# Half edge blocks instead of whole ones: how gathered rows are signalled, copied and awaited in a graph network on one core

## What is computed

```python
summed = jax.ops.segment_sum(h[src], dst, num_segments=N_NODES)   # three SAGE layers, a GCN of two, a GIN
msg_in = jnp.concatenate([nodes[row], nodes[col], edge_features], axis=-1)
messages = _mlp(msg_in, mW1, mb1, mW2, mb2)                       # the last network sums messages instead
aggregated = jax.ops.segment_sum(messages, col, num_segments=nodes.shape[0])
upd_in = jnp.concatenate([nodes, aggregated], axis=-1)
x = _layernorm(x + _mlp(upd_in, uW1, ub1, uW2, ub2))
```

## Time and profile before

| | |
|---|---|
| runs of the kernel | 5099.02 us median of 3 (5089.89 to 5105.0) |
| the profiled execution | 5097.06 us, of which the span from first to last instruction is 5095.3 us |
| busy share of the span | PE 82%, PEld 75%, DVE 64%, ACT 54%, POOL 65% |
| mean DMA traffic | 195 GB/s |
| stretches, us from the start | Sage0 111 to 940, Sage1 to 1642, Sage2 to 2235, Gcn1 to 2790, Gcn2 to 3388, Gin to 3974, Update to 5095 |

### The profile page before, as it was taken

One profiled execution on the slowest core, in us unless ns is written; L12 is line 12 of the kernel. 1 busy time (PEld: TensorE's weight loads), 2 busy tenths in 40 slices (PEclk: granted clock), 3 DMA queues, 4 the chain that ended last, 5 costly groups with the idle time before them and its releaser, 6 DMA issues. The chain is left out here.

```text
span 5095.3 us, 116107 instructions
## 1 busy us (share of the span) xinstructions
PE 4202.0 (82%) x31493; PEld 3798.6 (75%) x31494; DVE 3265.3 (64%) x6692; ACT 2762.0 (54%) x7100; POOL 3310.3 (65%) x3162
## 2 busy tenths in 40 slices
PE   2999999799997899979997455548888599999997
PEld 1899999799997888879997445536767366666665
DVE  5555555677775788857766566657777355555555
ACT  0566666455544777854443566655666244444444
POOL 2544443478773777747774777747775677777772
PEclk9999999899999999989999766679999799999999
DMA  1778787466665677758876566647777244444442
GB/s 35 214 250 252 252 252 248 173 232 242 231 235 211 224 257 261 259 197 275 279 266 232 162 184 184 190 143 216 224 210 205 74 118 117 117 119 119 119 115 89
DMA packets 490328, 991.07 MB, mean 195 GB/s; under 512 B 156821, under 2 KB 246965, under 8 KB 470968
## 3 DMA queue, kind: packets, MB, share of 16 engines
q1 hardware_dynamic: 389368, 872.44, 50.7%
q0 software_dynamic: 100800, 116.72, 11.4%
HBM read 452.18 MB, written 380.15 MB: 163 GB/s over the span
## 5 line engine op out<-in xcount | busy, mean ns | idle before, releaser
L753 PE MATMUL ps_all<-arena 128*128 x16000 | 2023.1, 286 | 501.8 <-DMA arena<-arena 348.3
L753 PEld LDWEIGHTS ps_all<-arena 128*128 128x128 f32 x16000 | 1989.8, 204 | 549.1 <-issue 545.5
L682 POOL DMA_INDIRECT arena<-n_t,ix_now x784 | 907.8, 1158 | 426.2 <-issue 401.1
L682 POOL DMA_INDIRECT arena<-y_t,ix_now x784 | 808.3, 1031 | 347.6 <-issue 329.6
L1132 ACT ACTIVATE arena<-bytes 128x2048 f32<-128x2048 uint8 (+1 forms) x300 | 475.8, 1618 | 381.9 <-DMA bytes<-pairs_d 215.8
L682 POOL DMA_INDIRECT arena<-x_rows,ix_now x392 | 373.7, 953 | 375.1 <-PE ps_all L753 263.7
L682 POOL DMA_INDIRECT arena<-x_t,ix_now x392 | 403.7, 1030 | 176.8 <-issue 166.4
L1667 PE MATMUL ps_all<-w,tp 128*128 128x128 f32 x4000 | 490.9, 276 | 28.8 <-ACT store_b L1810 28.2
L1667 PEld LDWEIGHTS ps_all<-w,tp 128*128 128x128 f32 x4000 | 477.9, 192 | 47.2 <-issue 38.6
L1097 ACT ACTIVATE bytes<-arena 128x1024 uint8<-128x1024 f32 (+1 forms) x200 | 296.8, 1484 | 242.3 <-DMA pairs_d<-bytes 240.5
L712 DVE TENSOR_TENSOR arena<-iota,window 128x1024 f32<-128x1024 f32 x302 | 363.3, 1219 | 100.8 <-ACT bytes L1097 93.9
(11 more groups left out here) (212 smaller groups left out, 7689.5 us busy)
## 6 DMA issues: line engine op xcount, KB each, us to landing
x_t<-store_a SPq DMA_DIRECT2D x150, 512.0 KB
s_t<-store_a SPq DMA_DIRECT2D x50, 1024.0 KB
n_t<-store_b SPq DMA_DIRECT2D x50, 1024.0 KB
load_a<-s_t SPq DMA_DIRECT2D x50, 1024.0 KB
bytes<-pairs_d SPq DMA_DIRECT2D x100, 512.0 KB
y_t<-store_b SPq DMA_DIRECT2D x100, 512.0 KB
load_b<-x_t SPq DMA_DIRECT2D x100, 512.0 KB
arena<-arena SPq DMA_DIRECT2D x147, 192.0 KB
```

Of the source, the lines that this page charges most:

```text
L682: pool.indirect_dma_start(out=slot_rows(at, W, pitch), out_offset=None, in_=table, in_offset=bass.IndirectOffsetOnAxis(ap=ix_now[:, at:at ...
L753: last = pe.matmul(out(j, 2) if wide else out(j, 1), hot, both(rows) if wide else rows, start=(k == 0), stop=(k == n - 1))
```

## The change

The rows of an edge block are treated as two halves h = 0 and 1 of four tiles (`HT`), each with semaphores of its own. POOL signals each half. PE waits at group 0 of node block m only for the second half of edge block m-1, and at group 1 for the first half of edge block m. `skewed` copies for node block m first the second half of edge block m-1 and then the first half of edge block m, each in nine transfers, behind a wait of its own for that half and for the sums of group 0 or 1. The check in the setup allows a tile's edges only up to where PE will have waited. On the drawn inputs, the quantity that it compares with its bound of 6 lies between -1 and 4.

```diff
-                step(V.tensor_scalar(sc_i[:, 1, :], sc_i[:, 0, :], 4, 3, ALU.logical_shift_right, ALU.logical_shift_left))
+                step(V.tensor_scalar(sc_i[:, 1, :], sc_i[:, 0, :], 3, 2, ALU.logical_shift_right, ALU.logical_shift_left))
...
-                step(V.tensor_scalar(sc[:, CC, :], sc[:, DD, :], float(2 * ET - 2), None, ALU.is_gt))
+                step(V.tensor_scalar(sc[:, CC, :], sc[:, DD, :], float(2 * HT - 2), None, ALU.is_gt))
...
         def block(m, v, i, c):
...
-            if not isinstance(m, int) or m >= 2:
-                pool.wait_ge(S(f"rows{v % 2}"), landed(f"rows{v % 2}", i - 1, ET))
             n = ET // len(parts)
             for k, summed in enumerate(parts):
+                name = f"rows{v % 2}{k * n // HT}"
+                if k * n % HT == 0 and (not isinstance(m, int) or m >= 2):
+                    pool.wait_ge(S(name), landed(name, i - 1, HT))
...
-        def rows_in(self, pe, m, i, u):
-            if not has_edges(m):
-                return
-            if self.two_windows:
-                pe.wait_ge(S(f"rows{u}"), landed(f"rows{u}", i, ET))
-            else:
-                pe.wait_ge(S(f"skew{u}"), landed(f"skew{u}", i, self.SKEW_DMAS))
+        def parts_of(self, m, i, u):
+            return ([(m - 1, i + u - 1, 1 - u, 1)] if exists_before(m) and has_edges(m - 1) else []), [(m, i, u, 0)] if has_edges(m) else []
+
+        def rows_in(self, pe, m, i, u, q):
+            if not exists_before(m):
+                q = 1
+            for e, n, v, h in self.parts_of(m, i, u)[q]:
+                if self.two_windows:
+                    pe.wait_ge(S(f"rows{v}{h}"), landed(f"rows{v}{h}", n, HT))
+                else:
+                    pe.wait_ge(S(f"skew{v}{h}"), landed(f"skew{v}{h}", n, self.SKEW_DMAS))
...
-            self.rows_landed(sp, m, i, u)
-            sp.sem_inc(S("copying"), 1)
-            if not isinstance(m, int) or m >= 2:
-                sp.wait_ge(S("agg0"), before(m - 1))
-            sp.sem_inc(S("copying"), 1)
-            W, at = self.pitch, (m % RB) * ET
-            last = (at + (RING - 1)) % RING
...
-            for k in range(1, SKEWS):
-                low = k * STEP
-                for a, b, to, source, n in ((low, P, at, at, ET), (0, low, at, at + 1, ET - 1), (0, low, last, at, 1)):
-                    sp.dma_start(arena[a:b, ring_of(k, to, n)], arena[a:b, ring_of(0, source, n)]).then_inc(S(f"skew{u}"), 16)
+            for q, part in enumerate(self.parts_of(m, i, u)):
+                for e, n, v, h in part:
+                    self.rows_landed(sp, e, n, v, h)
+                    sp.sem_inc(S("copying"), 1)
+                    if not isinstance(m, int) or m >= 2:
+                        sp.wait_ge(S(self.parts[q * len(self.parts) // 2]), before(m - 1))
+                        sp.sem_inc(S("copying"), 1)
+                    at = ((e + RB) % RB) * ET + h * HT
+                    last = (at + (RING - 1)) % RING
+                    for k in range(1, SKEWS):
+                        low = k * STEP
+                        for a, b, to, source, w in ((low, P, at, at, HT), (0, low, at, at + 1, HT - 1), (0, low, last, at, 1)):
+                            sp.dma_start(arena[a:b, ring_of(k, to, w)], arena[a:b, ring_of(0, source, w)]).then_inc(S(f"skew{v}{h}"), 16)
```

More of the change, by code:

```diff
@@ L74, in dram @@
         return nc.dram_tensor(name, shape, dt).ap()
-    sets = [[ctx.enter_context(nc.semaphore(f"set{k}_{i}")) for i in range((64, 77)[k])] for k in range(2)]
+    sets = [[ctx.enter_context(nc.semaphore(f"set{k}_{i}")) for i in range((66, 79)[k])] for k in range(2)]
     names, current = {}, [0]
     soft, base, first = {}, {}, [0]
-    POOL_DMAS = ("wing0", "wing1", "rows0", "rows1", "pair00", "pair01", "pair10", "pair11", "g_rows", "g_old", "g_put")
+    POOL_DMAS = ("rows00", "rows01", "rows10", "rows11", "g_rows", "g_old", "g_put")
     def kept(name):
@@ L494, in _ @@
                     last.then_inc(S("wint"), 1)
+        for u in range(2):
+            carry(f"rows0{u}", 32 * ((NW + 1 - u) // 2))
         pro.close()
@@ L611, in pass_over @@
             for u in range(2):
-                carry(f"rows{u}", 16 * ET * ((EB + 1 - u) // 2))
+                for h in range(2):
+                    carry(f"rows{u}{h}", 16 * HT * ((EB + 1 - u) // 2))
             carry("g_rows", 16 * z.etiles)
@@ L683, in block @@
                         out=slot_rows(at, W, pitch), out_offset=None, in_=table,
-                        in_offset=bass.IndirectOffsetOnAxis(ap=ix_now[:, at:at + 1], axis=0)).then_inc(S(f"rows{v % 2}"), 16)
+                        in_offset=bass.IndirectOffsetOnAxis(ap=ix_now[:, at:at + 1], axis=0)).then_inc(S(name), 16)
         for m in range(min(RB, EB)):
@@ L884, in lists_ahead @@
             for u in range(2):
-                sp.wait_ge(S(f"rows{u}"), landed(f"rows{u}", (EB + 1 - u) // 2 - 1, ET))
+                for h in range(2):
+                    sp.wait_ge(S(f"rows{u}{h}"), landed(f"rows{u}{h}", (EB + 1 - u) // 2 - 1, HT))
             for buf, ix in self.next_lists:
                 sp.dma_start(buf[:, :], ix[:, 0:2 * IX]).then_inc(S("next_lists"), 16)
-        rows_signal, rows_dmas, lists = "rows", ET, 1
+        rows_signal, rows_dmas, lists = "rows", HT, 1
         def next_index(self, sp, m, i, v):
@@ L895, in next_index @@
                 for k in range(2):
-                    name = f"{self.rows_signal}{k}"
-                    sp.wait_ge(S(name), landed(name, i, self.rows_dmas))
-                    sp.sem_inc(S("copying"), 1)
+                    for h in range(2):
+                        name = f"{self.rows_signal}{k}{h}"
+                        sp.wait_ge(S(name), landed(name, i, self.rows_dmas))
+                        sp.sem_inc(S("copying"), 1)
                 if not isinstance(c, int) or c >= 1:
@@ new lines, in rows_in, with rows_landed @@
+        def rows_in(self, pe, m, i, u, q):
[6 more added lines that the diff above has]
+                    pe.wait_ge(S(f"skew{v}{h}"), landed(f"skew{v}{h}", n, self.SKEW_DMAS))
+        def rows_landed(self, sp, e, n, v, h):
+            sp.wait_ge(S(f"rows{v}{h}"), landed(f"rows{v}{h}", n, HT))
@@ L1710, in build, with rows_landed @@
         consumed = ("hid3",)
-        def rows_landed(self, sp, m, i, u):
-            if isinstance(m, int) and m == 0:
+        def rows_landed(self, sp, e, n, v, h):
+            if isinstance(e, int) and e == 0:
                 sp.wait_ge(S("zeros"), before(3))
-            super().rows_landed(sp, m, i, u)
+            super().rows_landed(sp, e, n, v, h)
         def load_block(self, sp, m, u):
@@ L2046, in emit @@
             gathered = store_a
+            mine_in = ("g_old", "g_put")
             with nc.Block() as block:
@@ L2166, in _ @@
                     both_ways(pe, general, lambda: None)
+            for name in mine_in:
+                carry(name, 16 * 2 * HT * NB)
     class Update(Pass):
@@ L2176, in build @@
         MINE = GT * P
[L2177 removed]
+        rows_dmas, lists = 2 * HT, 2
         PAIRS = 4
@@ L2187, in pairs @@
             return store_b[h][:, (k - 2) * 512:(k - 1) * 512]
[L2189 to L2196, removed]
-                if not isinstance(c, int) or c >= 1:
-                    sp.wait_ge(S("ix"), landed("ix", c - 1, self.lists))
-                self.load_index(sp, c + 2)
         def edges(self, u):
@@ L2253, in block @@
                     if not isinstance(m, int) or m >= 2:
-                        pool.wait_ge(S(f"pair{u}{h}"), landed(f"pair{u}{h}", i - 1, 2 * HT))
+                        pool.wait_ge(S(f"rows{u}{h}"), landed(f"rows{u}{h}", i - 1, 2 * HT))
                     if not isinstance(m, int) or m >= self.PAIRS:
@@ L2383, in turn @@
             if kind == "m":
-                pe.wait_ge(S(f"pair{u}{c}"), landed(f"pair{u}{c}", i + 1, 2 * HT))
+                pe.wait_ge(S(f"rows{u}{c}"), landed(f"rows{u}{c}", i + 1, 2 * HT))
                 source = self.pairs((self.place + 2) % self.PAIRS, c)
@@ L2408, in products, with rows_landed @@
             tile_products(pe, tq[s], (wm2 if kind == "m" else wu2)[:, :], ps[6 + s]).then_inc(S(f"{kind}mm{s}"), 1)
-        def rows_landed(self, sp, m, i, u):
-            for h in range(2):
-                sp.wait_ge(S(f"msum{h}"), now(m))
+        def rows_landed(self, sp, e, n, v, h):
+            sp.wait_ge(S(f"msum{h}"), now(e))
         def collect(self, pe, m, i, u, q, places):
```

28 lines of the change are left out of this document (12 added, 16 removed).

## The result

The changed kernel took **5779.7 us** (median of 4 runs, 5776.5 to 5784.1) against 5099.4 us before: a ratio of **1.134** (95% interval 1.132 to 1.1355). The forecast was 5680 us, with a range of 5500 to 5850. The profiled execution has a span of 5774.8 us, 679.5 more than before.

What follows compares the result with a forecast made beforehand. SP's issuing of copies was taken to bound Sage0, Gcn2 and Gin: 569 for issuing less waits, + 41 for more waits and counting, - 26 at pass starts = +584 us on 5097.06, giving 5680 us, range 5500 to 5850.

Steps and rivals of the forecast that it cites:

- SP's issuing is the bound in Sage0, Gcn2 and Gin: SP's queue in three passes: 441 more copies each, 322 us more in Gcn2 and Gin, 353 in Sage0; chance 0.72.
- The size of a copy doesn't matter: On SP's queue, a copy of half the bytes costs as much as a whole one, 0.73 us.
- each pass gets longer by the extra issuing less all of SP's waits: In the passes SP bounds: Sage0 353 - 169 = +184, Gcn2 322 - 158 = +164, Gin 322 - 101 = +221 us.
- The cross-check from two turns: In Gin, a 9.31 us turn with nine more copies is 15.9 against a mean of 10.7: +250 us.
- rival B: PE's clock also falls in Sage0, to 0.69, so PE needs 1112 us there: 5765 us in all; chance 0.12.
- C: Less of SP's extra issuing comes through, without Sage0's +184 and half of the rest: 5300 to 5490 us; chance 0.09.
- E: Nothing happens: the setup's check blocks the window way, or SP's work is hidden: 5099 us; chance 0.03.
- Update 0: In Update, nine more copies, 6.6 us, fit into SP's 11 us a block of waiting for stores: 0 us.
- The transfers: On the DMA engines, 28,224 more packets a pass are at most 187 us of all 16, not the bound: 0.
- Rival D's 181 us: If issuing went by bytes, Gcn2's and Gin's turns would fall to 8.6 and 9.5 us: 4915 us; chance 0.04.
- The rule weighed: The Trainium skill's some 50 ns for a dispatch would make 441 copies 22 us, a gain; the trace disagrees.
- The signs: Profile after: PE's copy waits in Gcn2 and Gin well above 319 us; Sage1, Sage2 and Gcn1 within 5 us each.

Runs made afterwards that it cites:

- e4: The changed kernel with the one-tile and three-tile copies of each second half merged, 15 copies a block instead of 18: 5459 us.
- e2: The kernel before plus nine 1 KB copies for each edge block of Gcn2, Gin and Update, awaited by PE with the others: 5676 us.
- e9: The changed kernel with six gathers a block instead of eight in Gcn2 and Gin: 5784 us when run again.
- e5: e1_whole plus nine 1 KB copies for each edge block of Gcn2, Gin and Update: 5478 us.
- e1_whole: The changed kernel with whole edge blocks copied again in nine copies, which PE awaits at group 1 instead of group 0: 5065.4 us.
- e6: e1_whole with the loads of block m+2 ahead of the copies on SP's queue in Gcn2: 5064.2 us.

## Why the prediction was right, and where it was off

*SP's issuing is the bound in Sage0, Gcn2 and Gin*: right, and shown from three sides. Fewer issues with the same bytes give the time back at 0.70 us each (e4: 441 fewer issues in the three passes, 308 us). More issues with hardly any bytes cost it (e2). Taking work from POOL instead changes nothing (e9).

*The size of a copy doesn't matter*: right. 577 ns median for whole and half copies, 591 for 1 KB.

*The sum was 96 us too small*: +680 measured, +584 forecast. By passes: Sage0 +208 (forecast 184 + 14), Gcn2 +213 (164 + 14), Gin +267 (221 + 14), Update +11 (0), the starts and the passes without copies together -19 (-26). Two thirds of the miss are in Gcn2 and Gin, in the step "each pass gets longer by the extra issuing less all of SP's waits". SP's waits didn't all go. The rows of the waits count the first and last blocks of a pass too, where SP doesn't wait for a turn. After the change no wait for stores, gathers or loads is left within the loops of Gcn2 and Gin, but 25 us of the counted rows stayed at the ends of Gcn2 and 19 in Gin. The cross-check from two turns that began 9.31 us apart had said +250 for Gin, which is nearer the +267 than the number I kept. The other part is what lies between the two sets of a turn. Nine copies still take 6.6 us (0.73 each), but 18 take 13.7, and 13.7 - 2 x 6.58 = 0.54 us for the second set's waits and their counting, where I had 4 x 0.07 = 0.28. That is 13 us more in a pass. 25 + 13 and 19 + 13 account for the 35 and 32 us that were missing in Gcn2 and Gin. In Sage0 the 15.6 us that I had for 18 copies (8.4 for one set and 0.80 for each copy of the other) is what they took on the mean.

*The clock falls in Sage0 (rival B)*: it fell, from 1.00 to 0.94, and didn't reach the time: Sage0's PE has 840 us of work in 1037 us, and its turn of 20.5 us is SP's 15.6 us of copies and some 5 us for its five other transfers. C and E didn't happen.

*Update 0*: the number was right (+11). The reason given for it, that SP's idle time takes the copies in, is only half of it. e2 has the same idle time and pays 197 us. The other half, that PE sums the block a turn later, isn't enough by itself: in e2, with the old wait, PE waits 181 us for copies, and in e5, with the later one, 15. The changed kernel has later waits too, by half a block, and PE's wait for copies in its Update is 39 us (1.7 before).

*The transfers*: right that they are no bound, and the price for them was far too high. From the page's part 3 after:

```profile
q1 hardware_dynamic: 530488, 872.55, 45.0%
```

0.450 x 16 x 5774.8 = 41,579 us of packets against 0.507 x 16 x 5095.3 = 41,333. So 141,120 more packets with the same bytes cost 246 us of one DMA engine, 15 us of all 16, in the whole kernel. (The two shares are printed to 0.1%, so it may be anything from 160 to 330.) I had 28,224 more a pass (113,000 in four) and a bound of 187 us for each. The count was too low as well: 141,120 are 720 for each edge block of the four passes, where I had 576. The 144 between them are 16 for each of the nine further copies. The small copies of e2, of 32 partitions, fit this count: 63,504 more packets on this queue for 1323 copies are 48 each.

*Rival D's 181 us*: by POOL's pace they would not have been there even with copies for free, though no run had such copies. I had set POOL's floor in Gcn2 at its busy time, 8.6 us a block, and left out the 0.3 us gaps, although I had counted them in Update. With them it is 11 us, the turn that Gcn2 already had. With as many copies as before, the later wait is worth e1_whole's 34 us, of which 16 are in the passes without copies.

*The rule weighed*: the 50 ns that the prediction took from the Trainium skill (DMA: Bandwidth & Descriptors, Anatomy of one DMA) stand there for a transfer that POOL issues, and these copies are SP's. The runs have a median of 577 ns for them.

*The signs*: two of them failed. PE's wait for copies in Gcn2 and Gin was to be well above 319 us and is 175 + 128 = 303, since in Gcn2 most of PE's waiting has moved to the matrices (60 us before, 293 after), which wait for a load behind the copies. And Sage2 and Gcn1 were to stay within 5 us, but are 10 and 14 us shorter (593 to 583, 557 to 543), and 6 and 16 in e1_whole, though only 4.3 us at the start of each had been counted. What else PE's half waits save there stays open. The turns of Gcn2, Gin and Sage0 (15.8, 16.3 and 20.5 us against 14.7, 15.5 and 19.9) are longer by the terms above.

## What to carry to other kernels

Halving the unit of a signal also halves the unit of whatever is issued on that signal: count the instructions, not the bytes, and look at the issuing queue before looking at the DMA engines. The wait that gets looser can be had without splitting the transfers, by moving the wait to the later consumer. The two versions that do this and add no copies (e1, e6) are the only ones that gained with all the work done. When a wait goes and another of the same length comes (e1, e6), look for the engine with no rest at all, and count the gaps between its instructions as its work.

## What was not expected of the hardware

A copy inside SBUF held SP for a median of 0.57 to 0.59 us (0.50 at the least), from 1 KB to 192 KB, while Gcn2's transfers of 512 KB to or from DRAM held it for 0.35 (the rows of SP's order of time show both). POOL's gathers of 128 rows took 0.94 us at the least and 1.07 on the mean of the 300 us of e1_whole, with 0.30 us between two of them. Each copy inside SBUF has 16 packets beyond one for each of its partitions. 141,120 more packets for the same bytes took the DMA engines hardly more time: some 2 ns each (1.1 to 2.4).
